# A gather, Gram and MLP kernel on one core: eight places for gathered rows, MLP layers in small pieces, and a new split of the copying between ScalarE and VectorE

## The reference, cut to what matters

```python
e = jnp.stack([tbl_0[ids[:, 0]], ..., tbl_31[ids[:, 31]]], axis=1)   # (512, 32, 256) f32, a gather
iu, ju = jnp.triu_indices(32, k=1)
dots = jnp.einsum('bnd,bmd->bnm', e, e)
z = dots[:, iu, ju]                                                 # (512, 496)
h = jnp.concatenate([z, dense_ctx], axis=1)                          # (512, 512)
h = jnp.maximum(h @ W_top1 + b_top1, 0.0)                            # (512, 512)
h = jnp.maximum(h @ W_top2 + b_top2, 0.0)                            # (512, 256)
y = h @ W_top3                                                       # (512, 1)
```

## Time and profile before

| | us |
|---|---|
| median of 3 runs | 233.93 (232.72 to 234.01) |
| the profiled execution | 231.57 |
| its span, first to last instruction | 229.7 |
| PE busy in it | 151.3 |
| POOL busy in it | 122.6 |
| DVE busy in it | 75.2 |
| ACT busy in it | 63.7 |

### The profile page before, as it was taken

One profiled execution on the slowest core, in us unless ns is written; L12 is line 12 of the kernel. 1 busy time (PEld: TensorE's weight loads), 2 busy tenths in 40 slices (PEclk: granted clock), 3 DMA queues, 4 the chain that ended last, 5 costly groups with the idle time before them and its releaser, 6 DMA issues.

```text
span 229.7 us, 2734 instructions
## 1 busy us (share of the span) xinstructions
PE 151.3 (66%) x962; PEld 136.9 (60%) x962; DVE 75.2 (33%) x236; ACT 63.7 (28%) x190; POOL 122.6 (53%) x135
## 2 busy tenths in 40 slices
PE   0659005586648663956378999584755997669695
PEld 0448004586647563956276898473745996669594
DVE  0110003543516261526161007370617008264531
ACT  2101001433514151325141123250506035153441
POOL 3777763675757575757575034575757526510010
PEclk9999655579957995699887699979799589988999
DMA  1593331322323232333232102323232303210000
GB/s 46 136 365 110 98 114 46 93 80 81 113 71 109 79 103 79 96 88 94 83 99 77 37 26 62 98 90 96 83 101 75 108 9 96 82 49 0 0 0 3
DMA packets 7759, 18.80 MB, mean 82 GB/s; under 512 B 2593, under 2 KB 3489, under 8 KB 7618
## 3 DMA queue, kind: packets, MB, share of 16 engines
q0 software_dynamic: 6144, 16.79, 24.9%
q1 hardware_dynamic: 1602, 1.84, 2.6%
HBM read 18.62 MB, written 0.00 MB: 81 GB/s over the span
## 4 chain that ended last, share of the span: by engine, by line
PE 46%; another core or an unknown queue 19%; issue 10%; DVE 10%; ACT 8%; DMA 3%; POOL 2%; DVEq 0%; ACTq 0%
PE gram_ps L335 24%; PE xt_ps L314 7%; PE mlp_ps L380 7%; ACT z L187 5%; DVE slots L228 4%; PE mlp_ps L388 3%; DVE z L187 3%; ACT xt L209 3%; DMA rows<-in_table,row_number 2%; POOL rows L197 2%; PE mlp_ps L367 2%; DVE xt L209 2%; DVE slots L238 1%; DMA ids_sb<-in_ids 1%
## 5 line engine op out<-in xcount | busy, mean ns | idle before, releaser
L197 POOL DMA_INDIRECT rows<-in_table,row_number x128 | 121.7, 951 | 79.7 <-PE xt_ps L314 31.8
L335 PE MATMUL gram_ps<-xt 128*128 128x128 f32 x504 | 84.1, 320 | 65.0 <-DVE xt L209 23.9
L335 PEld LDWEIGHTS gram_ps<-xt 128*128 128x128 f32 x504 | 75.9, 230 | 71.9 <-issue 26.1
L209 DVE COPY xt<-xt_ps 128x512 f32<-128x512 f32 x32 | 22.1, 691 | 99.7 <-remote 47.9
L314 PE MATMUL xt_ps<-identity,rows 128*128 128x128 f32 x256 | 47.6, 315 | 10.5 <-DMA rows<-in_table,row_number 10.5
L314 PEld LDWEIGHTS xt_ps<-identity,rows 128*128 128x128 f32 x256 | 36.0, 164 | 13.0 <-issue 6.9
L209 ACT COPY xt<-xt_ps 128x512 f32<-128x512 f32 x31 | 18.2, 586 | 65.1 <-remote 34.5
L187 DVE COPY z<-slots 32x32 f32<-32x32 f32 x142 | 30.8, 217 | 2.3
L187 ACT COPY z<-slots 32x32 f32<-32x32 f32 x111 | 27.1, 244 | 9.6 <-DVE slots L238 6.9
L228 ACT COPY slots<-gram_ps 32x256 f32<-32x256 f32 (+1 forms) x32 | 11.6, 361 | 61.4 <-PE gram_ps L335 47.7
L228 DVE COPY slots<-gram_ps 32x256 f32<-32x256 f32 (+1 forms) x32 | 13.1, 410 | 11.3 <-PE gram_ps L335 8.0
(11 more groups left out here) (26 smaller groups left out, 22.5 us busy)
## 6 DMA issues: line engine op xcount, KB each, us to landing
rows<-in_table,row_number POOLq DMA_INDIRECT x128
w1z_sb<-in_w1z SPq DMA_DIRECT2D x1, 1024.0 KB
w_sb<-in_w SPq DMA_DIRECT2D x1, 512.0 KB
ids_sb<-in_ids SPq DMA_DIRECT2D x1, 64.5 KB, 1.9
identity<-in_eye SPq DMA_DIRECT2D x1, 64.0 KB, 2.1
upper_sb<-in_takes_upper SPq DMA_DIRECT2D x1, 64.0 KB
ctx_sb<-in_ctx_t SPq DMA_DIRECT2D x1, 32.0 KB
w1c_sb<-in_w1c SPq DMA_DIRECT2D x1, 32.0 KB
```

The source lines that it names most:

```text
L197: nc.gpsimd.indirect_dma_start(rows[:, n % RING, :], None, table, bass.IndirectOffsetOnAxis(ap=row_number[:, n:n + 1], axis=0),).then_inc( ...
L209: copy(xt[:, p % XT_RING], xt_ps[p % 2][:]).then_inc(xt_ready[p % 2], 1)
L335: done = nc.tensor.matmul(product_ps(n), x, x, start=(k == 0), stop=(k == KD - 1))
```

## The change

- `RING` goes from 16 to 8 places of `rows`.
- The row numbers are computed in two instructions: four tiles first, then the rest. POOL starts after the first.
- ACT copies all pairs from `xt_ps` to `xt`, DVE none (but for one of the last two tiles). DVE takes all four quadrants of each unit and spreads all 16 cells; ACT none, but for the last unit, which keeps its split. One semaphore `xt_ready` counts the pairs.
- Batches are (0, 32), (32, 32), (64, 32), (96, 32), each 128 samples wide. At `TURN[batch]` + n (n = 0 to 3) PE does one quarter of the first layer with its context product, and ACT one ReLU; the second layer follows at +4, the third at +5.
- `mlp_ps` has four 128-wide places in each of two banks.

```diff
-RING = 16
+RING = 8
-N = 256
+N = 128
+FIRST = 4
-BATCHES = [(0, 64), (64, 32), (96, 32)]
+BATCHES = [(0, 32), (32, 32), (64, 32), (96, 32)]
-DVE_CELLS, ACT_CELLS = CELLS[:9], CELLS[9:]
...
         @block.gpsimd
         def _(pool):
-            pool.wait_ge(numbered, 1)
             for n in range(TILES):
+                if n in (0, FIRST):
+                    pool.wait_ge(numbered, 1 if n == 0 else 2)
                 if n >= RING and n % 2 == 0:
                     pool.wait_ge(transposed, (n - RING) // 2 + 1)
...
         def take_blocks(engine, copy, quadrants, u, tiles, pairs, done):
             engine.wait_ge(gram_ready, pairs)
-            if u >= 2:
-                engine.wait_ge(z_dve, u - 1)
-                engine.wait_ge(z_act, u - 1)
...
             def unit(u):                                       # DVE
-                take_blocks(dve, nc.vector.tensor_copy, (0, 1), u, ALL, UNIT // 2 * (u + 1), blocks_ready)
-                take_upper(u, ALL, blocks_ready, 2 * (u + 1))
-                spread(dve, nc.vector.tensor_copy, DVE_CELLS, z_dve, u)
+                take_blocks(dve, nc.vector.tensor_copy, range(J), u, ALL, UNIT // 2 * (u + 1), blocks_ready)
+                take_upper(u, ALL, blocks_ready, u + 1)
+                spread(dve, nc.vector.tensor_copy, CELLS, z_dve, u)
...
             for p in range(LAST_PAIR):                         # DVE
-                if p % 2 == 0:
-                    copy_pair(dve, nc.vector.tensor_copy, p)
...
             for p in range(LAST_PAIR):                         # ACT
-                if p and ended_unit(p - 1) is not None:
-                    unit(ended_unit(p - 1))
-                if p % 2 == 1:
-                    copy_pair(act, nc.scalar.copy, p)
+                copy_pair(act, nc.scalar.copy, p)
                 for batch in range(LAST):
-                    if p == TURN[batch]:
-                        relu1(batch)
+                    if TURN[batch] <= p < TURN[batch] + KH1:
+                        relu1(batch, p - TURN[batch])
...
                 for batch in range(LAST):                      # PE
-                    if p == TURN[batch]:
-                        context(batch)
-                        z_complete(batch)
-                        for n in range(KH1):
-                            if n >= 2:
-                                pe.wait_ge(h1_ready, batch * KH1 + (n - 1))
-                            layer1(batch, n)
-                    if p == TURN[batch] + 1:
+                    n = p - TURN[batch]
+                    if 0 <= n < KH1:
+                        if n == 0:
+                            z_complete(batch)
+                        if n >= 2:
+                            pe.wait_ge(h1_ready, batch * KH1 + (n - 1))
+                        context(batch, n)
+                        layer1(batch, n)
+                    if n == KH1:
                         pe.wait_ge(h1_ready, batch * KH1 + KH1)
-                        for n in range(KH2):
-                            layer2(batch, n, range(KH1))
-                    if p == TURN[batch] + 2:
+                        for i in range(KH2):
+                            layer2(batch, i, range(KH1))
+                    if n == KH1 + 1:
                         layer3(batch)
```

More of the change, by code:

```diff
@@ L101, in dlrm_tower @@
         gram_ps = [psum(f"gram_ps{i}", [P, UNIT, J, F]) for i in range(2)]
-        mlp_ps = [psum(f"mlp_ps{i}", [P, 2, N]) for i in range(2)]
+        mlp_ps = [psum(f"mlp_ps{i}", [P, 4, N]) for i in range(2)]
         ids_loaded = sem("ids_loaded")
@@ L283, in _, with relu1 @@
         def _(act):
-            def relu1(batch):
+            def relu1(batch, n):
                 act.wait_ge(b1_loaded, 16)
-                for n in range(KH1):
[L287 to L293, removed]
+                act.wait_ge(h1_done, batch * KH1 + (n + 1))
+                nc.scalar.activation(h1_sb[:, n, 0:count(batch)], h1_ps(batch, n), ACT.Relu,
+                                     bias=b1_sb[:, n:n + 1]).then_inc(h1_ready, 1)
             for p in range(LAST_PAIR):
-                if p and ended_unit(p - 1) is not None:
-                    unit(ended_unit(p - 1))
-                if p % 2 == 1:
-                    copy_pair(act, nc.scalar.copy, p)
+                copy_pair(act, nc.scalar.copy, p)
                 for batch in range(LAST):
-                    if p == TURN[batch]:
-                        relu1(batch)
-            take_blocks(act, nc.scalar.copy, (2, 3), LAST_UNIT, FIRST_SIX, LAST_PAIR, blocks_ready)
+                    if TURN[batch] <= p < TURN[batch] + KH1:
+                        relu1(batch, p - TURN[batch])
+            act.wait_ge(z_dve, LAST_UNIT - 1)
+            take_blocks(act, nc.scalar.copy, (2, 3), LAST_UNIT, FIRST_SIX, LAST_PAIR, first_six_ready)
             copy_last(act, nc.scalar.copy, 1)
-            take_blocks(act, nc.scalar.copy, (2, 3), LAST_UNIT, LAST_TWO, PAIRS, last_blocks_ready)
+            take_blocks(act, nc.scalar.copy, (2, 3), LAST_UNIT, LAST_TWO, PAIRS, last_two_ready)
             spread(act, nc.scalar.copy, LAST_CELLS[1], z_act, LAST_UNIT)
-            relu1(LAST)
+            for n in range(KH1):
+                relu1(LAST, n)
         @block.tensor
@@ L353, in last_gram, with context @@
                 product(TILES - 1).then_inc(gram_ready, 1)
-            def context(batch):
+            def context(batch, n):
                 pe.wait_ge(ctx_loaded, 32)
[L357 to L362, removed]
+                if batch and n == 0:
                     pe.wait_ge(y_ready, batch)
-                for n in range(KH1):
-                    own_bank = batch == LAST or n < 2
-                    nc.tensor.matmul(h1_ps(batch, n), w1c_sb[:, n * P:(n + 1) * P],
-                                     ctx_sb[:, samples(batch)], start=own_bank, stop=False, skip_group_check=True)
+                nc.tensor.matmul(h1_ps(batch, n), w1c_sb[:, n * P:(n + 1) * P], ctx_sb[:, samples(batch)],
+                                 start=True, stop=False)
             def z_complete(batch):
@@ L373, in z_complete @@
                 pe.wait_ge(z_dve, (first + tiles) // UNIT)
-                pe.wait_ge(z_act, (first + tiles) // UNIT)
                 if batch == LAST:
+                    pe.wait_ge(z_act, 1)
                     pe.wait_ge(z_pool, 1)
@@ L424, in _ @@
             last_gram()
-            context(LAST)
+            pe.wait_ge(last_xt_ready[0], 1)
+            pe.wait_ge(last_xt_ready[1], 1)
+            pe.wait_ge(blocks_ready, LAST_UNIT)
+            for n in range(KH1):
+                context(LAST, n)
             for _ in range(WARM):
-                nc.tensor.transpose(mlp_ps[1][:, 1, 0:P], identity[:], identity[:])
+                nc.tensor.transpose(mlp_ps[1][:, 3, :], identity[:], identity[:])
             z_complete(LAST)
```

45 lines of the change are left out of this document (23 added, 22 removed).

## The result

The changed kernel takes 219.09 us (median of 4 runs, 217.87 to 219.66); the kernel before took 233.97 us on the same chip (4 runs, 232.72 to 234.47). The ratio is 0.952, with a 95% interval of 0.940 to 0.965: 4.8% faster. I predicted 217.0 us. The profiled execution is 219.66 us, span 217.9; my sum for it was 215.2. The times of one kernel spread within a set, the longer ones mostly at a lower granted clock; the ratios come from the shorter ones alone, and where it matters the fastest run is given beside the median.

The account below looks back on a forecast made before the run. GpSimd's gathers pace a chain, with pauses from late PE signals. Gathers 163.3, pauses 29.7, tail 20.3 and 1.9 around the span make 215.2 us, 217 on the runs' scale; own range 207 to 226, overall 182 to 226.

Parts of the forecast that it names:

- The bound: Whole kernel: a chain paced by GpSimd's gathers, 163.5 us without a pause, plus 38.3 us of pauses and a 27.9 us end.
- Eight places: Ring of `rows`: POOL stops at 23.2 instead of 33.2 us; the tail after the last issue is 20.3 us instead of 27.9.
- the four pairs: Tail after POOL's last issue: four pairs left instead of seven, 5.0 us at 1.33 with one clock rise.
- Layers in pieces: PE's layers: stalls of 8.74, 2.58, 5.55 and 0.9 us go, 16.6 us; new signals cost one pause a batch, 4.9 us.
- the start and thirteen cycles: POOL's pauses outside the layers: about 3.7 us at the start and 13 cycles of 1.62 us each, 21.1 us.
- the slack: Eight-place ring: 5 us left before a pair must be signalled, enough to hide 2.8 us of arrears from the layers' pieces.
- The split: ACT copies, DVE does units: DVE busy 88 us, a unit 5.6 us, ending before due; copies no longer wait 2 to 3 us.
- Rival 1: PE's signals: holding goes with the backlog, POOL runs through to 163.3; 181 us, 183 on the runs' scale; chance 0.22.
- Rival 2: POOL's pauses: every second one goes, 15 us, tail 18; 198 us, 200 on the runs' scale; chance 0.13.
- rival 3: Ring: too few places, a pause in each four tiles, 51.8 us; 237.3 us, 240 on the runs' scale; chance 0.10.
- Rival 4: DVE's spreading holds up POOL's issues for its full length, 22.8 us; 238 us, 240 on the runs' scale; chance 0.02.
- Rival 5: POOL's pauses: one is traded for another, 16 us of new ones instead of 4.9; time within 1%; chance 0.03.

Follow-up runs that it names:

- the control: The changed kernel with no edit, run in the third set on a chip where no signal is held: 180.08 us, ratio to the kernel before 0.970.
- the first set: Follow-up runs on one chip (kernel before 230.35 us): sixteen places 224.12, eight places in the kernel before 225.03, gap before each pair 247.54, no gathers 153.33 us.
- the other two sets: Follow-up runs on two further chips, no held signal in any trace; the kernel before took 186.97 us in the second set and 188.23 in the third.
- the third set: Runs on one chip (kernel before 188.23 us): changed kernel unedited 180.08, half of PE's product signals 180.2, old split 180.61, whole layers 199.36 us.

## Why the prediction was right, point by point

**The bound.** Right. POOL still paces the kernel, PE's signals are still held, and a release still comes with POOL's pause. The control experiments say more than I had known: without gathers, or with a gap before each pair, no signal is late. What I missed is that half of the pauses that are left (16.8 of 33.6 us) don't come from held signals.

**Eight places.** Right, in place and size: POOL stops at 23.1 (predicted 23.2), and the tail is 20.9 (predicted 20.3) against 27.9. The ring undone alone gave back the 27.9. The 0.6 us are in the four pairs, which I put at 5.0 although four times 1.33 is already 5.3.

**Layers in pieces.** The sum came right and its parts didn't; this is luck. I had 4.9 us at the layers, for PE's new signals being held, and 24.8 for the start and thirteen cycles, 29.7 together. Measured are 16.8 us at the layers, where PE was late and its signals were not, and 16.8 for the rest: 11.9 more and 8.0 less, so the total is off by only 3.9. Without the second error the sum would have been 227.1 us. The steps that failed are two that I had called hidden. First, the slack. I had 0.7 us of arrears in each of four pairs, from a quarter and a pair at full clock in 3.2 us, and for half the clock I counted nothing. PE was at half the clock in the first two quarters of two batches and in most of the first quarter of the third; a quarter and a pair then took 5.25 us, 2.7 more than POOL's 2.51 each, and the slack of 5 was gone (at full clock they took 2.83, better than I had thought). Second, the unit on DVE, under "The split". It remains right that the stalls of 8.74 and 5.55 us are gone and that no pause is over 3 us less the usual 0.30.

The scale helped too. I added 1.0% because the profiled execution before lay under the median; the one after is the longest of its four runs. So the forecast of 217.0 misses the median by 2.1 us, and the sum of 215.2 misses its own execution by 4.5: 3.9 of pauses and 0.6 of tail. My count (about 18 pauses of 1.6 to 2) was off in form: 15 are over 0.9, and 15 smaller ones come beside them.

**The split.** I had said that DVE's results are there before they are due, since the layers come two pairs later, 5.0 us at POOL's pace, and that I am wrong if a unit on DVE is what PE waits for before the layers. It is: 3.1 us before the second and the third batch's, 0.2 before the first's. After a release PE doesn't go at POOL's pace; it was through the two pairs 3.1 us after DVE had started, and the unit took 6.1 (I had 5.6). In the control, with nothing held, the wait is 1.1 us a batch; in the kernels with the old split PE never waits there. DVE was busy 91.0 us in all (predicted 88). Where signals are held the split's worth was not measured by itself; with pieces and numbering it was 4.0 to 6.2 us in the first set. On the chips without held signals it is worth nothing (180.61 and 180.08).

**Rival 1**, the signals no longer held: it didn't happen in the result, but its picture is what the other two sets show, with POOL's last issue at 163.1 (163.3) and a time of 180.1 (181 for the profiled execution). I had thought that the kernel's pattern would decide whether signals are held. First of all the chip or its condition does: the same kernel gave 219.1 and 180.1.

**Rival 2** (half of the pauses gone) and **rival 3** (too few places): neither came. There are 30 pauses, where rival 3 said 30 and more, but most are short, and their sum is 33.6 us and not 51.8. Fewer places do make a long stretch of PE dearer (11.18 us where it was 8.74), but in the kernel before they saved more than that (225.03 against 230.35).

**Rival 4**, DVE's copies between SBUF tiles delaying POOL's issues: fell. With 247 of them on DVE the mean issue is 949 ns, and 948 in the third set, where POOL never pauses. But the copies wait for the issues: their mean went from 217 to 223 and 231 ns, and it is 188 without gathers. The rows above show how: the median copy takes 189 ns with and without gathers, but the longest 447 with them and 269 without. In the control 44 of the 247 take over 300 ns, and each of the 44 ends 10 to 23 ns after an issue's end; the 98 copies that lie wholly in an issue's first 700 ns take at most 194. So a copy that would run into the last 0.3 us or so of an issue ends with it. This costs DVE some 10.6 us there (247 x 43 ns), and in the kernel after 8.6. The rule of the Trainium skill, "SBUF — State Buffer", section "Who interferes with whom", has either side block the other, whoever comes first; this trace agrees in that one waits for the other, but here it is VectorE that waits, and only for the end of an issue.

**Rival 5**, pauses traded within 1%: didn't come, but it was nearer than its price says. To keep the time it would have needed 16.4 us more than my 4.9, about 21 us at the layers and not 16. 16.8 came.

**What stays open.** What inside the chip holds PE's signals; why it does so on one chip and not on another; and the rule by which a certain signal is late (four in a cycle pass). The kernels meant for it (half the signals, the gap at each sixth tile) and those meant to part the change (old split, whole layers) ran only where nothing is held, so their forecasts for held signals stand untested. Why the kernel before takes 7 to 8 us more than the changed one there isn't shown either. In the third set, the only one where the changed kernel ran beside the others, none beats it.

## What to carry to other kernels

A ring that is longer than the slack needs doesn't speed up its pacemaker; it moves work that must be caught up behind the last issue, and the time from there to the end is where it is paid. A short ring in turn has less stock for a long stretch of other work on the consumer (11.18 us of standing still where it was 8.74); it paid here all the same. Cutting that stretch into pieces bounds each pause, but took nothing off their sum here (16.6 and 16.8 us), as a piece with the steady work beside it took 5.25 us at the lower clock against the pacemaker's 2.51: work out that sum at both clocks, and look at what else the first piece waits for. When a forecast comes true, compare its terms and not only the sum. And measure on more than one chip before a part is called worthless: the change was worth 4.8% on one and 3.0% on another.

## What the hardware showed that I had not expected

- The same kernel takes 219.1 us on one chip and 180.1 on another; the kernel before took 230.35, 186.97 and 188.23 us on three. The difference is POOL's pauses (33.6 us and none) and the tail (20.9 and 15.1 us).
- In the result and the first set, while GpSimd issued gathers one behind another, a finished PE instruction's signal reached ACT, DVE or POOL up to 14 us late (20.23 + 1.06 to 35.45, with 16 places). With gaps of 1.3 us between issues, one in each pair, none was late, with a gather still on its way in each. On the two other sets' chips none was late at all.
- A VectorE copy of 32x32 elements between SBUF tiles that runs into the end of a gather's issue ends 10 to 23 ns after it: 44 of 247 took over 300 ns in the control, and none without gathers.
- After the same landing POOL issues 0.6 us later than PE starts (163.18 and 162.56); 63 such waits cost 66.6 us.
- The same 32 matmuls of a first layer ran at 2.4 or at 1.2 GHz, from batch to batch and run to run. Spread between transposes and products they kept 2.4 GHz in the control's profiled execution, and its runs lie within 2.7 us instead of 19; in the kernel after, on another chip, most of the first two quarters ran at 1.2 GHz.
